# A routed layer with padded row buffers, and its scatter of token rows tied to the convolution's progress

## What is computed

```python
# first half: a recurrence along time, for each of 128 channels
xn = layernorm(x)
h = dA * h + dB * u[..., None]            # over 256 steps
y = einsum('dn,bdn->bd', C_param, h) + D_param * u
x1 = x + y @ W_out.T + b_out
# second half: a mixture of experts, 2 of 8 for each token, and a shared one
logits = layernorm(x1) @ gate_w.T
w = top-2 of softmax(logits), made to sum to 1
out = swiglu(x1, shared) + sum over e of w[:, e] * swiglu(x1, expert e)
```

## Time and profile before

| | |
|---|---|
| median of 3 runs | 1392.8 us (1391.08 to 1397.02) |
| the profiled execution | 1388.5 us |
| its span (first to last instruction) | 1386.7 us |
| busy share of PE, DVE, ACT, POOL over the span | 80%, 59%, 42%, 27% |
| layer 0, from the start to its last instructions | 0 to about 401 us |

### The profile page before, as it was taken

How to read it: one execution, slowest core, us unless ns; L and a number is a source line. 1 busy time by engine, 2 the same in 40 slices (tenths; PEclk the granted TensorE clock), 3 DMA queues, 4 the chain that set the end, 5 groups by cost and what they waited for, 6 DMA issues and landing times. The chain is left out here.

```text
span 1386.7 us, 27126 instructions
## 1 busy us (share of the span) xinstructions
PE 1107.5 (80%) x9081; PEld 651.1 (47%) x9081; DVE 813.8 (59%) x1544; ACT 587.8 (42%) x1027; POOL 368.9 (27%) x487
## 2 busy tenths in 40 slices
PE   5263757866486799998896999999998499999596
PEld 2130437856443355554463555555555145555342
DVE  8651423322165588884347666666666478887344
ACT  5100102422223366656223555555555066666364
POOL 1277102452502244444502000000000044444202
PEclk9575788997888699999897999999999589999898
DMA  9732485367165233330000000000006233322002
GB/s 224 120 101 71 125 250 154 101 203 203 49 197 187 64 94 89 91 91 24 0 0 0 1 0 0 0 0 0 0 0 231 80 86 92 91 80 75 1 1 61
DMA packets 171562, 112.31 MB, mean 81 GB/s; under 512 B 15951, under 2 KB 165075, under 8 KB 171490
## 3 DMA queue, kind: packets, MB, share of 16 engines
q1 hardware_dynamic: 167170, 102.90, 26.4%
q0 software_dynamic: 4320, 8.47, 1.8%
HBM read 72.25 MB, written 35.33 MB: 78 GB/s over the span
## 5 line engine op out<-in xcount | busy, mean ns | idle before, releaser
L1445 DVE TENSOR_REDUCE at_mx<-banks 128x12 f32<-128x1536 f32 x128 | 225.1, 1759 | 82.7 <-PE banks L1313 80.0
L1429 ACT ACTIVATE at_p<-banks 128x512 f32<-128x512 f32 x384 | 213.9, 592 | 80.2 <-PE banks L1322 79.6
L1279 POOL TENSOR_SCALAR_AFFINE_SELECT at_p<-at_p 128x512 f32<-128x512 f32 x256 | 162.9, 637 | 259.0 <-ACT at_p L1429 255.3
L1322 PE MATMUL banks<-at_qbl,at_kst 128*128 128x512 f16 x384 | 130.0, 391 | 16.7 <-ACT at_p L1429 15.1
L452 POOL DMA_INDIRECT expert_outs<-ex_x_lo,rows_back_to x71 | 69.7, 982 | 159.8 <-ACT ex_x_lo L521 141.2
L1675 PE MATMUL banks<-f_h_hi,w_hi_h 128*128 128x512 f16 x256 | 97.0, 379 | 0.0
L1676 PE MATMUL banks<-f_h_lo,w_hi_h 128*128 128x512 f16 x256 | 97.0, 379 | 0.0
L1677 PE MATMUL banks<-f_h_hi,w_lo_h 128*128 128x512 f16 x256 | 97.0, 379 | 0.0
L1270 POOL COPY at_va<-v_all 128x256 f32 (+1 forms) x32 | 12.7, 397 | 313.5 <-PEq L1296 313.5
L903 DVE TENSOR_TENSOR ex_h_sb<-ex_sg,banks 128x512 f32<-128x512 f32 (+1 forms) x52 | 35.2, 683 | 102.8 <-remote 46.6
L501 ACT ACTIVATE ex_sg<-banks 128x512 f32<-128x512 f32 (+1 forms) x52 | 31.0, 599 | 150.4 <-remote 80.0
(11 more groups left out here) (364 smaller groups left out, 2321.6 us busy)
## 6 DMA issues: line engine op xcount, KB each, us to landing
gate_up_then_toeplitz<-kernel_padded SPq DMA_DIRECT2D x16, 1024.0 KB
at_qst<-at_q_stacked SPq DMA_DIRECT2D x32, 256.0 KB, 3.0
at_ksc<-at_k_stacked SPq DMA_DIRECT2D x32, 256.0 KB, 3.2
at_kst<-at_k_stacked SPq DMA_DIRECT2D x32, 256.0 KB, 2.8
at_qbl<-at_q_stacked SPq DMA_DIRECT2D x128, 64.0 KB, 1.9
expert_rows<-no_row SPq DMA_DIRECT2D x1, 4615.0 KB, 29.2
ssm_powers<-expert_rows SPq DMA_DIRECT2D x17, 260.0 KB
gate_up_then_toeplitz<-expert_outs SPq DMA_DIRECT2D x16, 256.0 KB, 3.8
```

Source lines behind the costliest of these rows:

```text
L1279: pool.affine_select(out=blk, in_=blk, compare_op=ALU.is_ge, fill=0.0, base=0, pattern=[[0, 4], [1, P]], channel_multiplier=-1).then_inc(p ...
L1322: pe.matmul(o, kst[m][:, g, kt * P:kt * P + P], qbl[m][:, g, :, qt * P:qt * P + P], start=True, stop=True).then_inc(t_mm, 1)
L1429: act.activation(dst, k.ps[:, T_B[(g * 3 + n) % 2], :].rearrange("p (j q) -> p j q", j=4), ACT.Exp, scale=scale).then_inc(p_ready, 1)
L1445: dve.tensor_reduce(mx[:, :, g * 4:g * 4 + 4].rearrange("p n j -> p j n"), k.ps[:, 0:4, 0:3 * P].rearrange("p j (n t) -> p j n t", t=P), A ...
```

## The change

Rows of `expert_rows` are 144 numbers (576 bytes) apart instead of 130 (520 bytes); 14 of them are zeros that are sent and not read back. The fill of `expert_rows` comes from `h`, a buffer of the shared expert, which is free then: four pieces of 10,224 bytes for each partition instead of 9088 rows of 520 bytes. The row transfers stand in 16 groups of four, and from the fifth group on each waits for one more step of the convolution. All 16 steps of the convolution stand ahead of the experts. `ranks` has a bank of its own, and waits for the turned input instead of the copied kernel. `copy_y` moves from DVE to ACT; `residual` moves behind the eight chunks; `low_part(0)` and `low_part(1)` stand earlier. The output projection stands four quads earlier, and the later layers' weights are issued three at each quad.

```diff
-ROW = DM + 2
+ROW, SENT = DM + 16, DM + 2
-EARLY = 12
+    BLANK = BLOCKS * ROW // 4
+    no_row = h[:].rearrange("p a b c -> p (a b c)")[:, 0:BLANK]
-    ahead, totals = (k.ps[:, b, SEQ:SEQ + TILES * NE] for b in CB)
+    ahead, totals = (k.ps[:, RANKS, m * TILES * NE:(m + 1) * TILES * NE] for m in range(2))
-        c = q - 6
+        c = q - 2
# SP
-            sp.dma_start(rows_in.rearrange("(n p) w -> p n w", p=P),
-                         no_row[:].unsqueeze(1).to_broadcast([P, BLOCKS, ROW])).then_inc(rows_blank, 16)
-            sp.dma_start(w_out[:], d["W_outT"]).then_inc(wout_in, 16)
+            sp.dma_start(rows_in.rearrange("(p n) w -> p (n w)", p=P).rearrange("p (m w) -> p m w", m=4),
+                         no_row.unsqueeze(1).to_broadcast([P, 4, BLANK])).then_inc(rows_blank, 16)
-            for s in range(EARLY):
+            for s in range(STEPS):
                 toeplitz(s + 2)
                 store_y(s)
+            sp.wait_ge(map_ready, 1)
+            for m in range(2):
+                sp.wait_ge(y_stored[m], STEPS // 2 * 64)
+            load_y(0)
             for m in range(2):
                 sp.wait_ge(rows_sent[m], TILES * 16)
             for q in range(XR):
                 load_rows(q)
             for q in range(QUADS):
-                if late_step(q) is not None:
-                    toeplitz(late_step(q) + 2)
-                    store_y(late_step(q))
                 c = out_chunk(q + 1)
+                if c:
+                    load_y(c)
                 if q + XR < QUADS:
                     load_rows(q + XR)
-                if q == 9:
-                    for arrived, weights in k.late0: ...
+                for arrived, dst, from_dram in late[q * each_time:(q + 1) * each_time]:
+                    sp.dma_start(dst, from_dram).then_inc(arrived, 16)
# POOL
                     for t in range(m * TILES // 2, (m + 1) * TILES // 2):
+                        step = (n * TILES + t) // TPC - 3
+                        if t % TPC == 0 and step > 0:
+                            pool.wait_ge(c_mm, step)
                         pool.indirect_dma_start(...)
# ACT: copy_y(c - 3) behind the two silu of chunk c >= 3, copy_y(5) to (15) behind the chunks
# PE
-                pe.wait_ge(k_copied, 2)
+                pe.wait_ge(xT_ready, NCH)                # ranks
-            for s in range(NCH - 2, EARLY):
+            for s in range(NCH - 2, STEPS):
                 convolve(s)
-                if late_step(q) is not None:
-                    convolve(late_step(q))
# DVE
+                if g == 0 and it == 0:
+                    dve.wait_ge(rows_blank, 16)          # gated
+            low_part(0)                                  # ahead of gate_probabilities()
-                residual(c)                              # in the loop over chunks
-                if c >= 3:
-                    copy_y(c - 3)
+            for c in range(NCH):                         # behind add(7)
+                residual(c)
-                if late_step(q) is not None:
-                    copy_y(late_step(q))
```

More of the change, by code:

```diff
@@ L341, in load_rows @@
                     sp.wait_ge(ids_done, q - XR + 1)
-                src = rows_in[q * CHUNK:q * CHUNK + blocks(q) * P, :].rearrange("(b p) w -> p b w", p=P)
+                src = rows_in[q * CHUNK:q * CHUNK + blocks(q) * P, 0:SENT].rearrange("(b p) w -> p b w", p=P)
                 sp.dma_start(xg[:, q % XR, 0:blocks(q), :], src).then_inc(xg_in[q % XR], 16)
@@ L353, in _ @@
                 load_rows(q)
+            late = [(arrived, dst, from_dram) for arrived, weights in k.late0 for dst, from_dram in weights]
+            each_time = -(-len(late) // (QUADS - XR))
             for q in range(QUADS):
-                if late_step(q) is not None:
-                    toeplitz(late_step(q) + 2)
-                    store_y(late_step(q))
                 c = out_chunk(q + 1)
[L359 to L367, removed]
+                if c:
+                    load_y(c)
                 if q + XR < QUADS:
                     load_rows(q + XR)
-                if q == 9:
-                    for arrived, weights in k.late0:
-                        for dst, from_dram in weights:
-                            sp.dma_start(dst, from_dram).then_inc(arrived, 16)
+                for arrived, dst, from_dram in late[q * each_time:(q + 1) * each_time]:
+                    sp.dma_start(dst, from_dram).then_inc(arrived, 16)
                 if q == 11:
@@ L414, in _ @@
                       channel_multiplier=0).then_inc(ids_set, 1)
-            pool.memset(no_row[:], NO_ROW).then_inc(ids_set, 1)
+            pool.memset(no_row, NO_ROW).then_inc(ids_set, 1)
             pool.iota(marks_i[:, TILES + BLOCKS:], pattern=[[P, TILES]], base=0, channel_multiplier=1).then_inc(ids_set, 1)
@@ L420, in _ @@
             pool.memset(zero[:], 0.0).then_inc(zero_set, 1)
+            pool.memset(z[:, :, SENT:], 0.0).then_inc(ids_set, 1)
             pool.memset(k.zero16[:], 0.0)
@@ L505, in _, with copy_y @@
                 act.activation(kn[:, half, :], k.ps[:, KB[half], 0:SEQ], ACT.Copy).then_inc(k_copied, 1)
-            high_parts(1)
-            for n in range(NCH * IT):
-                silu(n)
+            def copy_y(s):
+                m = s % 2
+                act.wait_ge(c_mm, s + 1)
+                if s == 0:
+                    act.wait_ge(slots_ready, 2)
+                if s >= 2:
+                    act.wait_ge(y_stored[m], s // 2 * 64)
+                bank = k.ps[:, CB[m], :]
+                back = bass.AP(tensor=bank.tensor, offset=bank.offset + SEQ - 1,
+                               ap=[list(bank.ap[0]), [SEQ, 2], [-1, SEQ]])
+                act.activation(ysb[:, m], back, ACT.Copy).then_inc(y_copied, 1)
+            high_parts(1)
+            for c in range(NCH):
+                for it in range(IT):
+                    silu(c * IT + it)
+                if c >= 3:
+                    copy_y(c - 3)
+            for s in range(NCH - 3, STEPS):
+                copy_y(s)
             def rows_high(q):
@@ L637, in convolve @@
             def convolve(s):
-                m, bank = s % 2, conv_bank(s)
+                m, bank = s % 2, CB[s % 2]
                 if s == 0:
                     pe.wait_ge(u_ready, 2 * XQ)
-                    pe.wait_ge(slots_ready, 2)
+                    pe.wait_ge(k_copied, 2)
                 pe.wait_ge(t_in[m], s // 2 * 16 + 16)
                 if s >= 2:
-                    pe.wait_ge(y_copied, s - 1 if s < EARLY else s)
+                    pe.wait_ge(y_copied, s - 1)
                 for c in range(CH):
@@ L918, in add @@
                                   ALU.add).then_inc(acc_done, 1)
[L920 to L928, removed]
             def add_out(c):
                 dve.wait_ge(o_mm, c + 1)
+                dve.wait_ge(x_plus, 2 * c + 2)
                 xc = k.x[:, c * TPC:c * TPC + TPC, :]
@@ L968, in _ @@
             slots()
-            low_part(0)
+            low_part(1)
             low_parts(1)
@@ L980, in _ @@
                     low_part(c + 2)
-                if c == 3:
+                if c == NCH - 2:
                     map_blocks()
-                residual(c)
                 if c:
                     add(c - 1)
-                if c >= 3:
-                    copy_y(c - 3)
             add(NCH - 1)
-            dve.wait_ge(acc_done, NCH)
-            for s in range(NCH - 3, EARLY):
-                copy_y(s)
+            for c in range(NCH):
+                residual(c)
             rows_low(0)
```

24 lines of the change are left out of this document (13 added, 11 removed).

## The result

| | us |
|---|---|
| before, median of 4 runs | 1391.9 (1390.9 to 1397.0) |
| after, median of 4 runs | 1338.1 (1337.1 to 1340.2) |
| after / before | 0.959, 95% interval 0.956 to 0.962 |
| profiled execution of after; its span | 1340.2; 1338.4 |

The gain is 54 us, and the time lies 8 us under the forecast of 1346. Between the two profiled executions the gain is 48.3 us (1388.5 to 1340.2), where the sum of the terms said 46.5. Most of the 8 us is thus no term of the sum: I had put the median 4.3 us above the profiled execution, as it stood before, and after the change it stands 2.1 us under it.

The account below looks back on a forecast made before the run. Layer 0 was taken to be bound by PE crawling, with late semaphores, while POOL sends rows without pause. Terms summed to -46.5 from 1388.5 profiled, giving 1342.0; with 4.3 for the median, 1346 us, 8-in-10 range 1332 to 1378.

Parts of the forecast that it names:

- ranks and slots: Layer 0's start: with an own bank and a fill in larger pieces, ranks start at 44.9, not 51.4: -6.5 us.
- DVE up to step 0: Before the convolution: two `residual` leave DVE's path and one `low_part` moves into a gap: -3.5 us.
- steps 0 to 11: Convolution steps and chunks beside the row transfers: 117.7 us becomes 72.3 with transfers in groups, -45.4 us.
- steps 12 to 15: The last four convolution steps now stand ahead of the experts: 6.0 and three of 4.8 us, +20.4 us.
- SP between steps and quads: Last step to first turned rows: SP also waits for all stores and issues a read first, +3.7 us.
- quads: Expert quads: four steps leave them, -4.0 us, and PE's waits for convolution output go, -11.2; pace stays 7.8.
- every wait is binding: Row groups beside chunks and steps: a group lasts 5.1 us, a step 6 to 7, so each group waits.
- The zeros: Quads: 4 MB of zeros take 19 us against row loads' 15 us of slack; nothing put, up to +5 us.
- The padding cures it: Rival, 14%: the crawl came from 520-byte rows on odd places, so bursts are nearly free: 1336 us.
- A burst is not absorbed: Rival, 14%: PE crawls through all 5.1 us of each group; chunks take 10.7 us, seven steps 7.3: 1374 us.
- the slowing outlasts each group: Rival, 6%: PE stays slow 5.2 us more in each group; chunks take 15.8 us, steps 12.6: 1436 us.
- The early code block is still late: Rival, 8%: ranks stay at 51.4, +6.5 us, and late rows at the zeros add up to 5: 1353 to 1358.

Follow-up runs that it names:

- e7: The changed kernel, unchanged, run again: 1339.0 us in a session where the kernel before took 1394.9.
- e8: The changed kernel without the waits between groups of row transfers, rows still padded: 1383.6 us where the kernel before took 1394.9.
- e2: The changed kernel with its waits but rows of 520 bytes again: 1304.4 us where the kernel before took 1323.9.
- e3: The changed kernel with rows of 520 bytes and without the waits: 1305.8 us where the kernel before took 1323.9.
- e1: The changed kernel without the waits between groups, rows padded: 1302.4 us where the kernel before took 1323.9.
- e5: The changed kernel with the first sixteen row transfers also in groups of four that wait: 1304.5 us where the kernel before took 1323.9.
- e12: The changed kernel with output chunks projected four quads later and late weight loads issued at once, as before: 1321.5 us where the kernel before took 1324.7.
- e6: The kernel before, unchanged, run again: 1395.6 us, ratio 1.001 to the kernel before of that session.
- e10: The changed kernel with the first sixteen transfers in groups and each quad's transfers one by one: 1301.5 us where the kernel before took 1325.8.

## Why the prediction was right

The terms, from the profiled executions of before and after (both held):

| term | forecast | measured | read as |
|---|---|---|---|
| ranks and slots | -6.5 | -7.4 | 51.39 to 43.98 |
| DVE up to step 0 | -3.5 | -0.7 | ranks to step 0: 35.65 to 34.92 |
| steps 0 to 11 | -45.4 | -50.8 | 117.7 to 66.9 (78.90 to 145.78) |
| steps 12 to 15 | +20.4 | +22.4 | 145.78 to 168.18 |
| SP between steps and quads | +3.7 | +0.5 | 7.2 to 7.7 (168.18 to 175.9) |
| quads | -15.2 | -13.2 | first turned rows to last `down`, 153.4 to 140.2 |
| the rest of the kernel | 0 | +0.9 | 1021.4 to 1022.3 |
| sum | -46.5 | -48.3 | |

*Luck.* The forecast came true because the pair was timed in a held session. Nothing in the prediction says so: it has no term and no rival for the session, and in a free one the versions of the changed kernel take 1301.5 to 1305.8 us, 26 us and more below its range. The sum, too, is closer than its parts: they miss by -5.4 and -3.2 on one side and by +2.8, +2.0 and +2.0 on the other.

*The bound.* That PE crawls while POOL sends without a pause, and that this and not bandwidth or code loading sets steps 0 to 11, was right for the sessions of the first pair of kernels: e7 and e8 show it with three lines. It was half of the cause. The other half, the held session, was in no view of one profile, and no rival had it. In a free session the waits are worth next to nothing (e2, e3), and the versions of the changed kernel gain 18 to 24 us; the changed kernel itself was not timed in one.

*Ranks.* Right in size. The landing of the fill fell from 29.2 us to 17.2, by part 6 of the page of after:

```profile
expert_rows<-ex_h_sb SPq DMA_DIRECT2D x1, 5112.0 KB, 17.2
```

Whether the new form of the fill or the bank of their own moved the ranks was not run.

*DVE up to step 0.* The step was right and something else took its gain. The two `residual` are gone, and in the free sessions ranks and step 0 stand 32.4 us apart (e1, e2, e5): 3.3 less than before's 35.65, against 3.5 forecast. In the held ones the late semaphore of chunk 2's product adds 1.7 to 2.4 us of idle DVE. That the cause is the first sixteen transfers, which still go out in one piece, is argued and not shown: e5 ran in a free session only. I had read them as harmless, since the crawl of before was plain only from 80 on.

*Steps 0 to 11.* The term with the largest miss, 5.4 us, and all of it in the chunks. I gave each of chunks 3 to 7 1.0 us for its burst, halfway between nothing and the quads' 1.9; it is nothing here (6.00 us each from 86.50 to 110.51) and 0 to 0.3 in e7. By reading, and not by a run: a chunk is bound by PE's own work, so a semaphore that comes late within the burst finds nobody waiting, while a quad waits for ACT and DVE in turn. Most groups also end before their step does (at 99.32 the one beside the step whose records end at 100.09), so the semaphore that frees the next group rises in a pause. A PE-bound stretch was the right neighbour, not the quad. The steps behind the chunks were expected at 6.0 us each (4.8 and 1.2) and take 5.94 (119.60 to 143.35, four steps); by e2, free, they take 5.1 with the same transfers. By this pair rows and stores beside the loads would cost 0.3, and late semaphores 0.8, where I had 0.7 and 0.5. But the split is loose: the same four steps take 5.5 each in e7, held, and 4.6 to 5.3 in the other free runs. The prediction's "every wait is binding" was also wrong for three groups of twelve, so that eight transfers can stand together here. The lateness is plain where such a run overlaps the end of a step: 3.0 us for step 11 (145.78 to 148.75). In e2 there is none: step 11's records end at 140.67 and SP issues at 140.73.

```profile
139.97 0.70 PE L667 MATMUL banks<-gate_up_then_toeplitz,w_h 128*16 128x128 f32 x8
...
140.73 0.38 SPq L325 DMA_DIRECT2D gate_up_then_toeplitz<-kernel_padded  x1
```

The Trainium skill ("Perfetto Trace Analysis", Summary: the profiler window per engine type) says that a matmul's end is estimated and that the way of its semaphore is hidden from the profile. The traces agree: what is late here stands in no record of PE, and is only seen as the distance to the record of the engine that waited.

*Steps 12 to 15.* 2 us more than forecast. By reading, it is the last two groups, of which I had counted one: step 12 starts 3.0 us behind step 11's end (145.78 to 148.82), and the last group stands beside it.

*SP between steps and quads.* I took the 3.3 us between stores and read from a stretch amid the quads, where two row loads stand between them (the row of 247.51 is these loads, not the stores). Here the read is issued 1.3 us behind the last store (170.57 to 171.91), and the row loads follow it at once.

*Quads.* -13.2 of -15.2. The waits are gone, and e12 brings them back. That quads keep 7.8 us was right; that the burst is the cause was half right, again: in free sessions quads with the same burst of four take 5.86 us. The zeros, at which I put nothing, cost a little more than before: the hole beside them is 6.1 us, where it was 4.9 (e1, free: 5.9).

*The padding.* Nothing was expected of it, and nothing clear was found. The reason that the prediction gave against it does not hold as it stands. The Trainium skill ("DMA: Bandwidth & Descriptors", How a descriptor splits into AXI transactions) gives the 25 beats for a piece that starts 224 bytes behind a multiple of 256. At a pitch of 576 bytes three of four rows start off such a multiple, but at a pitch of 520 bytes 31 of 32 do. An estimate worked out from that page's rule for all these starts (if the buffer itself starts on a multiple) gives 21 beats a row with the padding and 20.5 without; no run shows beats.

*The rivals.* "The padding cures it": e8 has the padding and crawls. Whether the waits would do as well without the padding in a held session stays open. "A burst is not absorbed" and "the slowing outlasts each group": chunks of 6.0 us. The second of these saw a true thing: in e8 SP hears of step 0 7.8 us after the last transfer's issue. Behind the run of eight that tail is 1.7 us (the last one ends at 147.06, SP issues at 148.75). "The early code block is still late": ranks at 43.98.

## What to carry to other kernels

Where an engine's records thin out while another sends software transfers without a pause, give the transfers a place: groups of four, each tied to a step of the work beside them, took back 45 us where the engine was held (e7 beside e8) and cost nothing measurable where it was not (e2 beside e3). Pauses of 1.4 us between the groups were enough in the chunks. Look at how late a semaphore comes (the record of the waiting engine less the end of the record that it waits for) beside a stretch of the same kind of work, since a PE-bound chunk hides a lag that a chain through ACT and DVE passes on. And run the kernel before in every session with what is compared to it: 68 us of this kernel came and went with nothing changed in it.

## What the runs showed of the hardware that I had not expected

- The same kernel on the same chip took 1394.9 us in one session and 1326.7 in a later one. In the first, with 64 indirect transfers of POOL back to back, PE started 35 matmuls in 55 us (e6, at a granted clock of 0.53 of 2.4 GHz, near the lower level of 1.2); with the same transfers in a free session 425 (e3, 0.84). What holds PE in the one and not in the other no run here shows.
- In a held session the slowing builds up: none in the first records of step 0, about one matmul in 1.4 us some 36 us into the transfers (e8). Semaphores are late before that: 3.4 us some 17 us into the first sixteen of the changed kernel (69.13 to 72.54).
- A held session shows, to a microsecond or two, only beside transfers of rows by POOL: from the last `down` on the kernel takes 1023.0 us in e8, held, and 1023.2 in e1, free.
- The padding costs nothing that can be measured: kernels with rows of 576 bytes took 1301.5 to 1304.5 us (e1, e5, e10), those with rows of 520 bytes 1303.2 to 1305.8, free. The times speak, if anything, for a gain of a microsecond or two.
